# Attention loop of a seven-stage kernel: mask tile in four ScalarE steps and a VectorE difference, one turned tile copied by ScalarE, maxima in two parts

## What is computed

```python
val  = sin(pq) * cos(pk) + sin(pk) * cos(pz) + sin(pz) * cos(pq) - threshold   # per head, L x L
mask = sigmoid(val / (temperature + 1e-6))
scores = einsum('bhqd,bhkd->bhqk', Q, K) / sqrt(8) + 0.3 * log(mask + 1e-6)
out = einsum('bhqk,bhkd->bhqd', softmax(scores), V)
```

## Time and profile before

| | |
|---|---|
| median of 3 runs | 2513.75 us (2509.22 to 2514.84) |
| the profiled execution, its own time | 2516.16 us |
| its span, first to last instruction | 2514.3 us |
| mean granted TensorE clock | 0.885 |
| PE busy over the span | 1950.6 us (78%) |
| DVE (VectorE) | 1599.0 us (64%) |
| ACT (ScalarE) | 1240.2 us (49%) |
| POOL (GpSimd) | 1070.4 us (43%) |

### The profile page before, as it was taken

How to read it: one execution, slowest core, us unless ns; L and a number is a source line. 1 busy time by engine, 2 the same in 40 slices (tenths; PEclk the granted TensorE clock), 3 DMA queues, 4 the chain that set the end, 5 groups by cost and what they waited for, 6 DMA issues and landing times.

```text
span 2514.3 us, 43414 instructions
## 1 busy us (share of the span) xinstructions
PE 1950.6 (78%) x14880; PEld 1224.8 (49%) x14880; DVE 1599.0 (64%) x2479; ACT 1240.2 (49%) x2826; POOL 1070.4 (43%) x838
## 2 busy tenths in 40 slices
PE   2788888858888986588888873896687888884596
PEld 1555555424555553355555532683344644642485
DVE  6677777556899796677777736584443344335486
ACT  2466655438999795465555543343322222224242
POOL 2555555335777675445655515132231033003333
PEclk9799999886999798789999985798898999896798
DMA  6000000020000001000000021204000000000202
GB/s 213 2 1 1 2 2 2 1 83 16 24 20 24 18 25 41 1 1 2 2 1 2 1 71 62 56 22 142 0 0 0 1 0 0 0 0 14 66 22 67
DMA packets 43928, 63.32 MB, mean 25 GB/s; under 512 B 7504, under 2 KB 33488, under 8 KB 42736
## 3 DMA queue, kind: packets, MB, share of 16 engines
q1 hardware_dynamic: 39232, 51.96, 6.6%
q0 software_dynamic: 4544, 9.35, 1.2%
HBM read 45.26 MB, written 21.18 MB: 26 GB/s over the span
## 4 chain that ended last, share of the span: by engine, by line
issue 30%; PE 19%; DVE 5%; ACT 3%; DMA 1%; SPq 1%; POOL 1%; DVEq 0%; POOLq 0%; ACTq 0%
PE PS L1721 3%; PE PS L448 2%; PE PS L1703 2%; PE PS L1705 1%; PE PS L1704 1%; DVE arena L756 1%; PE PS L1711 1%; PE PS L482 1%; DVE arena L769 1%; ACT arena L635 1%; PE PS L500 1%; PE PS L318 1%; PE PS L471 1%; DMA arena<-sorted_x 1%; PE PS L412 1%
## 5 line engine op out<-in xcount | busy, mean ns | idle before, releaser
L1495 POOL TENSOR_TENSOR arena<-arena 128x1024 f32<-128x1024 f32 x128 | 299.6, 2362 | 131.7 <-ACT arena L1429 131.7
L947 POOL TENSOR_TENSOR arena<-arena 128x512 f32<-128x512 f32 x128 | 132.8, 1040 | 263.7 <-DVE arena L790 261.8
L635 ACT ACTIVATE arena<-PS,arena 128x128 f32<-128x128 f32 x512 | 180.3, 370 | 125.3 <-DVE arena L783 124.9
L318 PE MATMUL PS<-arena_r 128*128 128x512 f32 x216 | 125.5, 581 | 135.2 <-DVE arena L756 63.8
L756 DVE SCALAR_TENSOR_TENSOR arena<-PS,fcol,big 128x512 f32<-128x512 f32 x256 | 177.3, 741 | 53.9 <-ACT arena L611 46.1
L1403 PE MATMUL PS<-con,arena 128*128 128x128 f32 x1024 | 157.2, 298 | 48.4 <-DVE arena L1479 46.0
L1479 DVE COPY arena<-PS 128x512 f32<-128x512 f32 x256 | 165.6, 684 | 21.3 <-PE PS L1403 21.2
L1403 PEld LDWEIGHTS PS<-con,arena 128*128 128x128 f32 x1024 | 118.8, 150 | 121.3 <-issue 94.6
L1429 ACT ACTIVATE arena<-PS,arena 128x512 f32<-128x512 f32 x256 | 154.9, 688 | 43.8 <-DVE arena L1460 42.1
L1440 ACT ACTIVATE arena<-arena 128x512 f32<-128x512 f32 x256 | 162.5, 636 | 23.3 <-DVE arena L1467 17.2
L2023 POOL DMA_INDIRECT expert_y<-arena x78 | 74.7, 958 | 209.3 <-DVE arena L1982 205.6
(11 more groups left out here) (366 smaller groups left out, 4924.3 us busy)
## 6 DMA issues: line engine op xcount, KB each, us to landing
big<-in_gu SPq DMA_DIRECT2D x16, 512.0 KB, 8.4
sorted_x<-in_slots SPq DMA_DIRECT2D x2, 2515.5 KB, 15.5
arena<-sorted_x SPq DMA_DIRECT2D x6, 774.0 KB, 7.6
big<-in_dn SPq DMA_DIRECT2D x16, 256.0 KB, 8.7
arena<-expert_y SPq DMA_DIRECT2D x16, 256.0 KB, 3.3
big<-in_wqkv SPq DMA_DIRECT2D x2, 1536.0 KB, 8.2
arena<-q_split SPq DMA_DIRECT2D x96, 32.0 KB
arena<-k_split SPq DMA_DIRECT2D x96, 32.0 KB
```

What stands on the lines that cost most here:

```text
L318: pe.matmul(bank, w_hi, hi, start=first, stop=False)
L635: act.activation(pr[:, u % 2, t, :], PS[:, u % 2, t * P:(t + 1) * P], ACT.Exp, bias=nmax[:, u % 2, t:t + 1], accum_out=psum_[:, u % 2, t:t ...
L947: g.tensor_tensor(pn[:, u % 2, :, :], pr[:, u % 2, :, :], pinv[:, u % 2, :].unsqueeze(2).broadcast_to([P, TPB, P]), ALU.mult).then_inc(s(" ...
L1495: g.tensor_tensor(a, a, mk[:, hp, 2 * half:2 * half + 2, :], ALU.mult).then_inc(s("a_masked"), 1)
```

## The change

The mask factor is formed as exp(0.3 (ln(1 + 1e-6 (1 + e^z)) - ln(1 + e^z))), with `c_one_more` = 1 + 1e-6 as a bias column. ScalarE does exp, ln(1 + .) into a new buffer `mk_ln`, ln(1e-6 . + 1 + 1e-6), and later the exponential; VectorE does the difference (new L1498). In the loop the difference and the last exponential of mask tile q = st+5 are placed in `scored(st+2)`, one step after the tile's other three operations: on VectorE behind the reductions, on ScalarE behind the four score exponentials (new L1440). POOL waits for `mask_done`, which the last exponential signals. VectorE's reduction is two, of two tiles each, and the exponentials of a half wait for its reduction. The copy of turned tile 3 goes from VectorE to the end of ScalarE's step (new L1477), with a semaphore `ppT_last` of its own. The counts of the semaphores that later stages reuse are adapted.

```diff
@@ -148,9 +148,9 @@
-                   "unit_down": ("a_pv", passes), "unit_high": ("a_nmax", passes), "unit_low": ("mask_arg", passes),
-                   "unit_out": ("mask_stage", 5 * passes), "unit_in_high": ("mask_clamped", passes),
-                   "unit_in_low": ("o_copied", passes), "hidden_turned": ("ppT_ready", TPB * passes),
+                   "unit_down": ("a_pv", passes), "unit_high": ("a_nmax", 2 * passes), "unit_low": ("mask_arg", passes),
+                   "unit_out": ("mask_stage", 3 * passes), "unit_in_high": ("mask_clamped", passes),
+                   "unit_in_low": ("o_copied", passes), "hidden_turned": ("ppT_ready", 3 * passes),
...
@@ -1045,8 +1045,9 @@
+            v.memset(c_one_more, 1.0 + 1e-6).then_inc(s("columns"), 1)
...
@@ -1138,6 +1139,7 @@
         a_nmax = carve([2, TPB])
+        mk_ln = carve([2, L])
         o_sb = carve([2, B, P])
...
@@ -1289,7 +1291,7 @@
-        MASK_OPS = 5
+        MASK_OPS = 3
...
@@ -1398,14 +1400,20 @@
                     if t % 2 == 0:
                         pe.wait_ge(s("a_masked"), START + at(i, 2 * STEPS, 2 * st + t // 2 + 1))
 
-                    pe.wait_ge(s("ppT_ready"), START + at(i, TPB * STEPS, TPB * st + t - 1) if st or t or type(i) is not int else START)
+                    if t >= 2:
+                        pe.wait_ge(s("ppT_ready"), START + at(i, 3 * STEPS, 3 * st + t - 1))
+                    elif t == 0:
+                        pe.wait_ge(s("ppT_ready"), START + at(i, 3 * STEPS, 3 * st))
+                    else:
+                        pe.wait_ge(s("ppT_last"), START + at(i, STEPS, st))
                     for kt in range(TPB):
                         tr = pe.transpose(PS[:, 4 + t % 2, kt * P:(kt + 1) * P], pp[:, st % 2, t, kt * P:(kt + 1) * P], ident)
                     tr.then_inc(s("a_transposed"), 1)
 
             def values(i, st):
                 hp, b = st // B, st % B
-                pe.wait_ge(s("ppT_ready"), START + at(i, TPB * STEPS, TPB * st + TPB))
+                pe.wait_ge(s("ppT_ready"), START + at(i, 3 * STEPS, 3 * st + 3))
+                pe.wait_ge(s("ppT_last"), START + at(i, STEPS, st + 1))
                 pe.wait_ge(s("v_head_ready"), START + at(i, HEADS_PER_PASS, hp + 1))
                 pe.wait_ge(s("o_copied"), START + at(i, STEPS, st))
 
@@ -1417,27 +1425,42 @@
 
             stepping(pe, scored, quarter, values, turned)
 
+        def later(i, k, by):
+
+            return i + (k + by) // STEPS, (k + by) % STEPS
+
         def attn_act(act):
             act.wait_ge(s("mask_rows"), START + 2)
 
+            def finished(i, q):
+                if type(i) is int and i >= PASSES:
+                    return
+                act.wait_ge(s("mask_difference"), START + at(i, STEPS, q + 1))
+                z = mk[:, q // TPB, q % TPB, :]
+                act.activation(z, z, ACT.Exp, scale=0.3).then_inc(s("mask_done"), 1)
+
             def scored(i, st):
                 for t in range(TPB):
+                    if t % 2 == 0:
+                        act.wait_ge(s("a_nmax"), START + at(i, 2 * STEPS, 2 * st + t // 2 + 1))
                     if t == 0:
-                        act.wait_ge(s("a_nmax"), START + at(i, STEPS, st + 1))
                         if st >= 2 or type(i) is not int or i:
                             act.wait_ge(s("a_transposed"), START + at(i, TPB * STEPS, TPB * (st - 1)))
                     act.activation(pp[:, st % 2, t, :], PS[:, t, :], ACT.Exp, bias=a_nmax[:, st % 2, t:t + 1]).then_inc(s("a_exp"), 1)
+                finished(*later(i, st, 3))
 
             def quarter(i, q):
 
                 hp, tile = q // TPB, q % TPB
                 act.wait_ge(s("mask_clamped"), START + at(i, STEPS, q + 1))
-                z = mk[:, hp, tile, :]
-                for k, (func, bias, scale) in enumerate(((ACT.Exp, 0.0, 1.0), (ACT.Ln, 1.0, 1.0), (ACT.Exp, 0.0, -1.0),
-                                                         (ACT.Ln, c_1e6, 1.0), (ACT.Exp, 0.0, 0.3))):
-                    if k:
-                        act.wait_ge(s("mask_stage"), START + at(i, MASK_OPS * STEPS, MASK_OPS * q + k))
-                    act.activation(z, z, func, bias=bias, scale=scale).then_inc(s("mask_stage"), 1)
+                z, n = mk[:, hp, tile, :], at(i, MASK_OPS * STEPS, MASK_OPS * q)
+                act.activation(z, z, ACT.Exp).then_inc(s("mask_stage"), 1)
+                act.wait_ge(s("mask_stage"), START + n + 1)
+                act.activation(mk_ln[:, q % 2, :], z, ACT.Ln, bias=1.0).then_inc(s("mask_stage"), 1)
+                act.wait_ge(s("mask_stage"), START + n + 2)
+                act.activation(z, z, ACT.Ln, bias=c_one_more, scale=1e-6).then_inc(s("mask_stage"), 1)
+                if type(i) is int and i == 0 and 1 <= q < TPB:
+                    finished(0, q - 1)
 
             def values(i, st):
                 act.wait_ge(s("a_pv"), START + at(i, STEPS, st + 1))
@@ -1447,17 +1470,32 @@
                 act.activation(o_sb[:, hp, b, :], PS[:, 6, 0:P], ACT.Copy).then_inc(s("o_copied"), 1)
 
             act.preload_act_table_set("natural_log_exp_and_others")
-            stepping(act, scored, quarter, values, nothing)
+            def turned(i, st):
+                t = TPB - 1
+                act.wait_ge(s("a_pv"), START + at(i, STEPS, st))
+                act.wait_ge(s("a_transposed"), START + at(i, TPB * STEPS, TPB * (st + 1)))
+                act.activation(ppT[:, :, t * P:(t + 1) * P], PS[:, 4 + t % 2, :].rearrange("p (a b) -> p a b", a=TPB),
+                               ACT.Copy).then_inc(s("ppT_last"), 1)
+
+            stepping(act, scored, quarter, values, turned)
 
         def attn_dve(v):
             v.wait_ge(s("a_values"), START + B + 2)
             v.wait_ge(s("mask_rows"), START + 2)
 
             def scored(i, st):
-                v.wait_ge(s("a_scores"), START + at(i, TPB * STEPS, TPB * (st + 1)))
-
                 v.wait_ge(s("a_exp"), START + at(i, TPB * STEPS, TPB * (st - 1)) if st or type(i) is not int or i else START)
-                v.tensor_reduce(a_nmax[:, st % 2, :], PS[:, 0:TPB, :], AX.X, ALU.max, negate=True).then_inc(s("a_nmax"), 1)
+                for t in (0, 2):
+                    v.wait_ge(s("a_scores"), START + at(i, TPB * STEPS, TPB * st + t + 2))
+                    v.tensor_reduce(a_nmax[:, st % 2, t:t + 2], PS[:, t:t + 2, :], AX.X, ALU.max, negate=True).then_inc(s("a_nmax"), 1)
+                difference(*later(i, st, 3))
+
+            def difference(i, q):
+                if type(i) is int and i >= PASSES:
+                    return
+                v.wait_ge(s("mask_stage"), START + at(i, MASK_OPS * STEPS, MASK_OPS * (q + 1)))
+                z = mk[:, q // TPB, q % TPB, :]
+                v.tensor_tensor(z, z, mk_ln[:, q % 2, :], ALU.subtract).then_inc(s("mask_difference"), 1)
 
             def quarter(i, q):
                 hp, tile = q // TPB, q % TPB
@@ -1466,6 +1504,8 @@
                     v.wait_ge(s("a_masked"), START + at(i, 2 * STEPS, 2 * B * (hp - 1)))
                 v.tensor_scalar(mk[:, hp, tile, :], PS[:, 7, :], acol[:, 5:6], MASK_CLAMP, ALU.mult,
                                 ALU.min).then_inc(s("mask_clamped"), 1)
+                if type(i) is int and i == 0 and 1 <= q < TPB:
+                    difference(0, q - 1)
 
             def turned(i, st):
                 hp, b = st // B, st % B
@@ -1474,7 +1514,7 @@
                     h = i * HEADS_PER_PASS + hp
                     plain_wait(v)
                     v.tensor_copy(v_head[:, hp, :, 0:HD], v_all[:, :, bass.ds(h * HD, HD)]).then_inc(s("v_head_ready"), 1)
-                for t in range(TPB):
+                for t in range(TPB - 1):
                     v.wait_ge(s("a_transposed"), START + at(i, TPB * STEPS, TPB * st + t + 1))
                     v.tensor_copy(ppT[:, :, t * P:(t + 1) * P],
                                   PS[:, 4 + t % 2, :].rearrange("p (a b) -> p a b", a=TPB)).then_inc(s("ppT_ready"), 1)
@@ -1484,15 +1524,18 @@
         def attn_pool(g):
             for b in range(B):
                 split_parts(g, b, 1, "a_split_k")
-            with g.Fori(0, PASSES) as i:
+            def one(i):
                 for st in range(STEPS):
                     hp = st // B
                     if st % B == 0:
-                        g.wait_ge(s("mask_stage"), START + at(i, MASK_OPS * STEPS, MASK_OPS * TPB * (hp + 1)))
+                        g.wait_ge(s("mask_done"), START + at(i, STEPS, TPB * (hp + 1)))
                     for half in range(2):
                         g.wait_ge(s("a_exp"), START + at(i, TPB * STEPS, TPB * st + 2 * half + 2))
                         a = pp[:, st % 2, 2 * half:2 * half + 2, :]
                         g.tensor_tensor(a, a, mk[:, hp, 2 * half:2 * half + 2, :], ALU.mult).then_inc(s("a_masked"), 1)
+
+            with g.Fori(0, PASSES) as i:
+                one(i)
 
 
         def attn_out_pe(pe):
```

(9 more changed lines are left out.)

## The result

| | before | after |
|---|---|---|
| median of 4 runs | 2511.56 us (2509.22 to 2514.84) | **2608.24 us** (2605.97 to 2610.80) |
| profiled execution, its own time | 2516.16 us | 2610.8 us |
| mean granted TensorE clock | 0.885 | 0.854 |
| attention loop, first to last step's reduction | 573.7 to 976.5 us | 573.5 to 1073.3 us |

The ratio is 1.0385 (95% interval 1.0361 to 1.0408): slower, by 96.7 us. One more run of the kernel before is counted here, which puts its median 2 us under the one that the prediction used. The loop grew from 402.8 to 499.8 us, by 97.0: all of the loss lies there.

A forecast was written before the change was run, and what follows sets the result against it. VectorE's chain through PE was taken as the bound, 5.86 us a step, ScalarE level with it. 2514 us plus 71 for clock falls and 29 for stalls at new heads gave 2614 us, range 2538 to 2690.

The forecast's parts named there:

- Ordinary step 6.11: Attention loop, VectorE's chain through PE: an ordinary full-clock step takes 6.11 us after the change, against 5.86.
- faster rival: Attention loop: ScalarE was the bound and loses its tight mask chain, 5.44 against 5.86 a step, 2489 us; chance 6%.
- Copy of tile 3 at 0: End of ScalarE's step: the moved copy hides behind the next scores, priced at 0, other end 0.2 a step.
- Copy of the head's values, +1.45: VectorE at each new head: the copy falls inside a POOL multiply with about 1.5 us left, +1.45 over 0.22.
- The rival that it would meet POOL at rest: New head: the head's values copy avoids POOL's multiply, only +0.3 to +0.5 a head, 2520 us; chance 8%.
- Even without the late start: New head: the head's values copy meets POOL's multiply even if POOL's first multiply does not wait for mask_done.
- Difference, 1.2 once per head: VectorE in a head's second step: the difference meets POOL's late multiply, 1.2 us instead of 0.69, +0.5.
- PE's wait of 2.3: PE at each new head: stands still some 2.3 us once per head; the head costs +2.4 us in sum.
- 12 falls of 20 us: Attention loop: stalls at 12 of 15 head changes start half-clock stretches of 20 us each, net +71 us.
- the forecast's price of 0.40: Attention loop: each us at half clock loses 0.40 us, from 30.8 us that lost 12.3.
- Collisions with the clock as before: Attention loop: stalls come but only two half-clock stretches, 13 heads x 2.4 = +31, 2545 us; chance 17%.
- Half clock throughout: Attention loop: half clock in nearly every step, up to +238, taken as +225, 2739 us; chance 8%.

The follow-up runs named there:

- Number 8: Kernel before with the mask part alone (four ScalarE steps, difference, mask_done), whole maxima and all four tile copies on VectorE: 2639.13 us, ratio 1.0499.
- Number 6: Kernel before with maxima in two reductions and the head's values copy on VectorE directly behind the reductions: 2473.42 us, ratio 0.9852.
- number 9: Kernel before with only the copy of turned tile 3 moved to ScalarE, keeping five mask operations: 2655.10 us, ratio 1.0558.
- number 3: Kernel before with only the maxima split into two reductions: 2600.87 us, ratio 1.0374.
- number 2: Changed kernel with four unused matmuls on PE between turns of tiles 1 and 2 in each head's first step: 2544.32 us, ratio 1.0149.
- number 1: Changed kernel with the head's values copy on ScalarE, ahead of the copy of tile 3, instead of VectorE: 2532.85 us, ratio 1.0096.
- number 7: Changed kernel with the head's values copy on VectorE directly behind the reductions, ahead of the difference: 2599.54 us, ratio 1.0352.
- number 4: Kernel before with maxima in two reductions and the head's values copy at the end of ScalarE's step: 2562.28 us, ratio 1.0223.
- number 5: Kernel before with maxima in two reductions, head's values copy on ScalarE behind the output copy of the previous head's last step: 2484.97 us, ratio 0.9895.

## Why the prediction was right

Forecast 2614 us, measured 2608.24; +100 forecast on the profiled execution, +96.7 measured on the medians. The mechanism came as forecast; that the total fits to 6 us is partly luck, since its two terms were off by some 9 and 6 us in opposite directions (below). By its steps:

- **Ordinary step 6.11**: measured 6.09 to 6.10 at full clock. Number 8 measures the difference alone, 0.61, none of it hidden. The faster rival (ScalarE the bound, 2489 us) is out: ScalarE waits for the reductions, 0.56 in the step that begins at 808.45 (first row below). Number 6 shows what it had right: without the difference, and with both collisions avoided, the maxima in two parts do shorten the step, to 5.74.
- **Copy of tile 3 at 0**: it fits the sum, since PE waits 0.36 for it and the step is 6.10, as the other terms give it. No kernel had the change without this copy, so the 0 is argued, not shown. It holds only beside the rest of the change: alone the copy costs 5.6% (number 9).
- **Copy of the head's values, +1.45**: 1.71 or 1.72 in place of 0.22 in 13 of 16 heads, 2.20 in two, so +1.50. The rival that it would meet POOL at rest (2520 us) is out. "Even without the late start" is borne out by number 3.
- **Difference, 1.2 once per head**: 1.08 to 1.31 in 12 heads, 0.68 otherwise. In an ordinary step it does not wait, but POOL does, which the forecast left out: the difference starts at 828.70, POOL's first multiply at 829.03, and that takes 2.58 instead of 2.36 (second row below). POOL has the slack for it. The next multiply behind a collision was forecast to be held up by 0.35; it is 0.45 (2.81).
- **PE's wait of 2.3**: 2.55 in the step shown. In number 2 the four steps of a head without a fall take 26.6 to 26.9, collisions included, against 24.1 before: +2.6, where the forecast has +2.4.
- **12 falls of 20 us**: 14, of 17 us on average, nine of them of only 10.2. More of them, but shorter, make nearly the same product: 238.5 us against 240. At the forecast's price of 0.40 they give its term, (238.5 - 61.4) x 0.40 = 71. The price itself came out lower: the loops of the changed kernel and of number 2 differ by 499.8 - 430.8 = 69.0 us for 197.6 us at half clock, 0.35, and a head with one stretch of 10.2 takes 30.3 where number 2 takes 26.7. By 0.35 the clock is 62 of the 97 us, not 71, and the stalls are 35, not 29: they count in nearly all 15 heads (15 x 2.4 = 36), where the forecast counted 12. The two errors nearly cancel.
- **Collisions with the clock as before (2545 us)**: its condition was nearly made by hand in number 2 (40.9 us at half clock instead of 61.4), which gave 2544.32. Its profiled loop grew by 28.0 us; 15 heads x 2.4 less (61.4 - 40.9) x 0.40 for the clock is 28 too. So the size of the stalls was about right. That the median meets the rival's figure within 1 us is luck: the rest of that profiled execution is 7 us shorter than the same part before, and the median is 7 us above it.
- **Half clock throughout (2739 us)**: out. At 1.00 in the last 345 us of number 6's loop the turns of tiles take about 2.2 of each 5.8 us. So the rule of the Trainium skill ("TensorE: Matmul & The Clock Gate", "Part 4: PE-mode transpose") does not decide here.
- **A slip in a reading**: the first of the 31 waits of 2.0 to 3.5 us is one of 3.02 that ends at 57.45, not the one that ends at 96.23. The counts of 31 and 22 are right, and nothing hangs on the first.

```profile
809.71 2.42 ACT L1449 ACTIVATE arena<-PS,arena 128x512 f32<-128x512 f32 x4 [0.56 <-DVE arena L1490]
...
829.03 2.58 POOL L1535 TENSOR_TENSOR arena<-arena 128x1024 f32<-128x1024 f32 x1 [3.92 <-ACT arena L1449]
```

Two mechanisms are shown by experiment: the collision with POOL (numbers 1, 3, 6, 7) and its price through the clock (number 2). The Trainium skill, "SBUF — State Buffer", section "Who interferes with whom", describes the first: VectorE's operations with two inputs in SBUF, and its copies in a mode that uses two ports, contend with POOL for a port pair, and of such a copy and POOL the one that issues first has the pair for the whole instruction. The traces agree, though none shows which mode the copy is in: in the changed kernel and in numbers 2, 3, 7 and 8 every lengthened copy of the head's values ends 0.08 to 0.09 us behind the end of one of POOL's multiplies, and every lengthened difference 0.55 behind one, however long it waited.

What stays open: why a stretch at 1.2 GHz lasts 10.2 us in most heads and 37.5 in others, and how the 21 us that number 1 still loses divide between the difference and its ten falls. Neither was tried by itself. A kernel with the change's mask steps and no late POOL, and the change without the copy of tile 3 on ScalarE, were not tried either.

## What to carry to other kernels

An operation of VectorE between SBUF and SBUF has a place in POOL's timetable, not only in VectorE's: a shift of POOL by about a microsecond (here exponentials that start earlier, or one mask operation that ends later) turned a copy of 0.22 into 1.7 to 2.2. So look for the few rare operations of a loop and place them where POOL rests, or on ScalarE, but there not at the end of a step without a gap (numbers 4 and 9). Price a stall of TensorE twice, once for itself and once for the clock behind it; here the second was twice the first. Parts that lose when taken alone need not add up: 3.7, 5.0 and 5.6% made 3.85% together, and moving the one copy turned the first of them into a gain of 1.5%.

## What the runs showed that was not expected

- A stop of TensorE of 1.48 us once per head, in an otherwise tight loop, was enough for 14 falls of the clock (number 4), and with the copy moved both the stop and these falls were gone (number 5); the prediction had put the danger at 2 to 3.5 us. Before the change both falls began in steps with a wait of about 1.0.
- Filling the wait with 1.99 us of matmuls kept the clock at 0.95 through the loop (number 2); the step is 8.26, 2.2 over an ordinary one.
- An instruction that clears POOL's multiply only just can hand the collision to its successor at a higher price: 0.75 and 2.85 in place of 1.72 and 1.22 (number 7).
- The copy of the head's values on ScalarE takes 0.29 to 0.34 in all three kernels that have it there, with no case like the 1.7 to 2.2 of VectorE.
